# An adaLN block on one core: the probabilities of tiles 8 and 16 turned by a trip over DRAM instead of by TensorE

## What is computed

```python
mod = (_silu(L0_c) @ L0_wmod).reshape(L0_c.shape[0], 6, 1, -1)      # sa, ca, ga, sb, cb, gb
h = _layernorm(x, axis=-1) * (1 + ca) + sa
x = x + ga * _L0_attn_ref(h, L0_attn_Wq, L0_attn_Wk, L0_attn_Wv, L0_attn_Wo)
h = _layernorm(x, axis=-1) * (1 + cb) + sb
x = x + gb * _L0_ffn_ref(h, L0_ffn_factors, L0_ffn_bias)
```

## Time and profile before

| | us |
|---|---|
| median of 3 runs | 449.46 (448.65 to 449.9) |
| the profiled execution | 449.87 |
| its span in the trace | 448.1 |
| PE busy | 439.6 (98%) |
| DVE busy | 357.2 (80%) |
| ACT busy | 321.0 (72%) |
| POOL busy | 235.3 (53%) |

### The profile page before, as it was taken

How to read it: one execution, slowest core, us unless ns; L and a number is a source line. 1 busy time by engine, 2 the same in 40 slices (tenths; PEclk the granted TensorE clock), 3 DMA queues, 4 the chain that set the end, 5 groups by cost and what they waited for, 6 DMA issues and landing times.

```text
span 448.1 us, 7294 instructions
## 1 busy us (share of the span) xinstructions
PE 439.6 (98%) x2118; PEld 361.5 (81%) x2118; DVE 357.2 (80%) x610; ACT 321.0 (72%) x642; POOL 235.3 (53%) x308
## 2 busy tenths in 40 slices
PE   8899999999999999999999999999999999999996
PEld 7586888878888888878888888888888888787885
DVE  5687657768887889978897888888886788999977
ACT  3677557778797786788877787778887673767651
POOL 1453516852565645355565545455564526077982
PEclk9999999999999999999999999999999999999999
DMA  8999976533676467667676367766676047558423
GB/s 317 392 385 290 251 151 111 125 120 98 195 221 191 132 195 229 200 181 242 194 250 191 116 203 234 223 192 220 199 236 210 25 152 207 183 173 278 130 79 140
DMA packets 77750, 88.05 MB, mean 197 GB/s; under 512 B 5000, under 2 KB 55944, under 8 KB 77200
## 3 DMA queue, kind: packets, MB, share of 16 engines
q1 hardware_dynamic: 73872, 80.51, 56.4%
q0 software_dynamic: 3264, 6.29, 7.8%
q10 hardware_dynamic: 576, 0.79, 0.5%
HBM read 53.49 MB, written 34.10 MB: 195 GB/s over the span
## 4 chain that ended last, share of the span: by engine, by line
PE 75%; DVE 11%; issue 4%; ACT 3%; POOL 3%; DMA 2%; DVEq 0%; POOLq 0%; SPq 0%
PE ps_o L524 9%; PE ps_o L526 9%; PE ps_o L525 9%; PE ps_v L524 6%; PE ps_v L525 5%; PE ps_v L526 5%; PE ps_y L526 4%; PE ps_y L524 4%; PE ps_y L525 4%; PE ps_qk L524 3%; PE ps_qk L525 2%; PE ps_qk L526 2%; PE ps_s L603 2%; PE ps_s L604 2%; DVE pt_lo L1194 2%
## 5 line engine op out<-in xcount | busy, mean ns | idle before, releaser
L1674 POOL TENSOR_SCALAR ve<-mv 128x1 f32<-128x1 f32 x64 | 16.5, 257 | 159.2 <-DVE mv L1309 118.2
L524 PE MATMUL ps_o<-v_lo,pt_hi 128*128 128x512 f32 x192 | 74.8, 389 | 0.6 <-DVE pt_lo L1194 0.6
L525 PE MATMUL ps_o<-v_hi,pt_lo 128*128 128x512 f32 x192 | 74.7, 389 | 0.0
L526 PE MATMUL ps_o<-v_hi,pt_hi 128*128 128x512 f32 x192 | 74.7, 389 | 0.0
L1194 DVE TENSOR_TENSOR h_lo<-h_f,h_hi 128x512 fp32r<-128x512 f32 x57 | 41.7, 731 | 28.7 <-ACT h_hi L832 28.4
L860 ACT ACTIVATE h_f<-x1b,mod_t 128x128 f32<-128x128 f32 x120 | 53.2, 596 | 3.8 <-DVE x1b L1327 3.8
L1676 POOL TENSOR_TENSOR rstd<-ve,minus_half 128x1 f32<-128x1 f32 x64 | 46.5, 727 | 5.3
L524 PE MATMUL ps_v<-wvo_lo,h_hi 128*128 128x512 f32 x112 | 44.7, 399 | 0.7 <-DVE h_lo L1194 0.7
L525 PE MATMUL ps_v<-wvo_hi,h_lo 128*128 128x512 f32 x112 | 43.7, 391 | 0.0
L526 PE MATMUL ps_v<-wvo_hi,h_hi 128*128 128x512 f32 x112 | 43.7, 390 | 0.0
L524 PEld LDWEIGHTS ps_o<-v_lo,pt_hi 128*128 128x128 f32 x192 | 36.0, 188 | 8.5 <-issue 1.0
(11 more groups left out here) (232 smaller groups left out, 1191.3 us busy)
## 6 DMA issues: line engine op xcount, KB each, us to landing
x_blocks<-xn SPq DMA_DIRECT2D x50, 256.0 KB, 2.7
p_blocks<-probs SPq DMA_DIRECT2D x24, 512.0 KB, 3.7
pb<-p_blocks SPq DMA_DIRECT2D x96, 128.0 KB, 2.8
x1b<-x_blocks SPq DMA_DIRECT2D x30, 256.0 KB, 2.8
result<-x_ring SPq DMA_DIRECT2D x15, 512.0 KB, 3.0
xb<-x_blocks SPq DMA_DIRECT2D x20, 256.0 KB, 3.0
x_ring<-in_x SPq DMA_DIRECT2D x18, 256.0 KB, 3.9
wmod<-in_wmod SPq DMA_DIRECT2D x4, 1024.0 KB, 15.7
```

Source lines behind the costliest of these rows:

```text
L524: nc.tensor.matmul(acc, a_hi, b_lo, start=first, stop=False)
L525: nc.tensor.matmul(acc, a_lo, b_hi, start=False, stop=False)
L526: return nc.tensor.matmul(acc, a_hi, b_hi, start=False, stop=last)
L1674: nc.gpsimd.tensor_scalar(ve[:, one], mv[:, u, 1:2], EPS, None, ALU.add).then_inc(ve_done, 1)
```

## The change

Tiles 8 and 16 are turned by the trip (`opens_by_trip`); tile 24 stays with PE. In steps 7 and 15 the scores of the opening tile stand ahead of the feed-forward, and DVE takes qk_lo and k_both (the keys' rests) directly behind the residual sum. Its exponential stands first among what ACT does behind the two pt_hi, and send and fetch are moved forward in SP's order. In steps 7, 8, 15 and 16 ACT handles x's columns (modulate, round) ahead of x1's. In steps 8 and 16 DVE turns the probabilities directly behind the first row maximum.

```diff
@@ -24,7 +24,11 @@
 
 
 def turned_by_pe(t):
-    return t <= LAST_EARLY or t % PER_BATCH == 0
+    return t <= LAST_EARLY or t == TILES - PER_BATCH
+
+
+def opens_by_trip(t):
+    return t % PER_BATCH == 0 and not turned_by_pe(t)
 
 
 def pe_turns_of(t):
@@ -454,19 +458,25 @@
                     fetch_x(t + TB + 1, 1 - u)
                 if opening is not None:
                     send_p(opening)
-                if t + 1 < T and not turned_by_pe(t + 1):
+                if t + 1 < T and not turned_by_pe(t + 1) and not opens_by_trip(t + 1):
                     fetch_p(t + 1)
+                if opens_by_trip(t + 1):
+                    send_p(t + 1)
                 if 1 <= t < T - 1:
                     send_x1(t - 1, 1 - u)
-                if u and g >= 2:
+                if opens_by_trip(t + 1):
+                    fetch_p(t + 1)
+                if u and g >= 2 and not opens_by_trip(t + 1):
                     store_pair(g - 2)
                 if 1 <= t < T - 1:
                     fetch_x1(t - 1, 1 - u)
+                if opens_by_trip(t + 1):
+                    store_pair(g - 2)
                 if t < T - TB and t % TB in (2, 4):
                     spread_gate(t % TB // 2 - 1, t // TB + 1)
                 if 12 <= t + TB + 2 < T:
                     send_x(t + TB + 2, u)
-                if scored_in(t) is not None and not turned_by_pe(scored_in(t)):
+                if scored_in(t) is not None and not turned_by_pe(scored_in(t)) and not opens_by_trip(t + 1):
                     send_p(scored_in(t))
                 if 2 * TB <= t + TB + 3 < T and t >= 5:
                     sp.wait_ge(y_stored, 16 * ((t - 5) // 2 + 1))
@@ -694,9 +704,11 @@
                     late_x()
                 if t:
                     project_values(t + TB, u)
+                if opens_by_trip(t + 1):
+                    scores_of(t + 1)
                 if t >= 3:
                     feed_forward(t - 3)
-                if scored_in(t) is not None:
+                if scored_in(t) is not None and not opens_by_trip(t + 1):
                     scores_of(scored_in(t))
                 if ready is not None:
                     ready()
@@ -994,6 +1006,8 @@
                 if scored_last_in(t - 1) is not None:
                     exponentials(scored_last_in(t - 1))
                 probs_part(t, 0)
+                if opens_by_trip(t):
+                    probs_part(t, 1)
                 if u:
                     qk(g + PB)
                 if q in late_x_banks:
@@ -1003,20 +1017,28 @@
                 if parts is not None:
                     parts(0)
                 values(t + TB)
-                probs_part(t, 1)
+                if not opens_by_trip(t):
+                    probs_part(t, 1)
+                if opens_by_trip(t + 1):
+                    exponentials(t + 1)
                 if parts is not None:
                     parts(1)
-                if t:
+                around = opens_by_trip(t) or opens_by_trip(t + 1)
+                if t and not opens_by_trip(t):
                     normalize_x1(t - 1, 1 - u, q < T)
-                if t >= 3:
+                if t >= 3 and not around:
                     modulate_x1(t - 2, batch_of((t - 2) // 2))
                 if q < T and q not in late_x_banks:
                     modulate_x_turned(q, batch_of(q // 2))
                 if q < T and t != 2:
                     h_upper(q, 1 - u)
+                if opens_by_trip(t):
+                    normalize_x1(t - 1, 1 - u, q < T)
+                if around:
+                    modulate_x1(t - 2, batch_of((t - 2) // 2))
                 if beside is not None:
                     beside()
-                if scored_in(t) is not None:
+                if scored_in(t) is not None and not opens_by_trip(t + 1):
                     exponentials(scored_in(t))
                 if behind is not None:
                     behind()
@@ -1336,25 +1358,38 @@
                 q = t + TB + 1
                 if scored_last_in(t - 1) is not None:
                     row_max(scored_last_in(t - 1))
+                if opens_by_trip(t):
+                    turn_p(t)
                 if t:
                     add_x(t - 1)
+                if opens_by_trip(t):
+                    probs_rest(t, 0)
+                    probs_rest(t, 1)
+                if opens_by_trip(t + 1):
+                    qk_rest(g + PB)
+                    k_rest(g + PB)
+                if t:
                     x1_stats(t - 1, 1 - u)
-                if u:
+                if u and not opens_by_trip(t + 1):
                     qk_rest(g + PB)
                 if t >= 3:
                     turn_x1(t - 2)
-                if u:
+                if u and not opens_by_trip(t + 1):
                     k_rest(g + PB)
-                probs_rest(t, 0)
+                if not opens_by_trip(t):
+                    probs_rest(t, 0)
                 if t == 2:
                     h_rest(q, 1 - u)
                 if between_halves is not None:
                     between_halves()
-                probs_rest(t, 1)
+                if not opens_by_trip(t):
+                    probs_rest(t, 1)
                 values(t + TB)
+                if opens_by_trip(t + 1):
+                    row_max(t + 1)
                 if q < T and q not in late_x_banks:
                     turn_x(q)
-                if scored_in(t) is not None:
+                if scored_in(t) is not None and not opens_by_trip(t + 1):
                     row_max(scored_in(t))
                 if t == 2:
                     turn_x1(0)
@@ -1369,7 +1404,7 @@
                     x_moments(q + 1, u)
                 if q < T and t != 2:
                     h_rest(q, 1 - u)
-                if not turned_by_pe(t + 1):
+                if not turned_by_pe(t + 1) and not opens_by_trip(t + 1):
                     turn_p(t + 1)
                 if t >= 2:
                     h2_rest(t - 2)
```

## The result

| | before | after |
|---|---|---|
| median, us | 449.50 (448.65 to 449.90, 4 runs) | 455.68 (455.04 to 456.19, 4 runs) |
| ratio, 95% interval | | 1.0134 (1.0106 to 1.0161) |
| profiled execution, its span | 449.87, 448.1 | 456.19, 454.4 |

A forecast was written before the change was run, and what follows sets the result against it. PE, busy 98% of the span, was taken as the bound. Around tile 8 +1.15 and tile 16 +1.8, the 1.76 gain included, make +2.95 on 449.46: 452.4 us, range 449.0 to 455.4.

The forecast's parts named there:

- 0.88 us a tile won: On PE, removing a tile's eight transposes saves 0.88 us, 1.76 us for both tiles.
- The trip of tile 8 is just hidden: Step 8: turned probabilities arrive at 161.7, DVE comes to them at 161.75; the trip costs 0 to 0.2 us.
- DVE's lateness in step 8: ACT idles until 152.2; h2_lo starts at 158.5, not 156.27, and the row maximum at 160.6, not 158.75.
- h_lo of tile 17 ends at 170.9, wait 1.2: Step 9: PE wants h_lo at 169.7 for queries and keys, so it waits 1.2 us, more than the 0.88 gained.
- The probabilities of tile 9 are there soon enough: Their send goes out about 2 us later than 161.24; they land at about 171, in time for what follows.
- The first pt_lo of tile 9 takes 0.69: Step 9 on DVE: starts 178.7, ends 179.4, making the attention of tile 9 1.05 us late.
- Tile 16, 1.8 us: Around tile 16 PE ends 1.8 us later, with no wait there to absorb any of it.
- 0.66 us absorbed at step 11: PE's earlier 0.66 us wait before step 11's queries and keys absorbs part of 1.8 us, leaving +1.15 around tile 8.
- The lateness and its cause: DVE's queue is late by 1.9 us from ACT's idle stretch and 1.17 us from the turn of the probabilities.
- Draw: Rival: only step 9's wait at the queries comes, 1.2 against 0.88, DVE catches up; 449.4 us; chance 0.19.
- full gain: Rival: the chains have slack, no waits come; 447.7 us, half of it 448.6; chance 0.15 in full or part.
- late trip: Rival: tile 8's probabilities land after DVE reaches them, 2.15 us late; 456.7 us, or 454.6 for one tile; chance 0.08.

The follow-up runs named there:

- e13: Changed kernel with ACT modulating x1's columns ahead of the exponential of tiles 8 and 16 in steps 7 and 15; ratio 1.0123 to the kernel before.
- e16: e13 with SP's store ahead of fetching tile 8's probabilities, and the send of tile 9's probabilities ahead of fetching x of tile 17; ratio 1.0137.
- e4: Changed kernel with SP's store of the finished pair put ahead of the fetch of the opening tile's probabilities; ratio 1.0121 to the kernel before.
- e5: Changed kernel with POOL's operations for tile t-4 held back in steps 9 and 17 until both pt_lo are done; ratio 1.0131 to the kernel before.
- e3: Changed kernel with eight dummy matmuls ahead of PE's wait for h_lo in step 9; ratio 1.0134 to the kernel before.
- e7: Changed kernel with the new order kept but no trip, PE transposing tiles 8 and 16 again; ratio 1.0113 to the kernel before.
- e17: e16 with the first pt_lo ahead of x1's statistics on DVE in steps 9 and 17; ratio 1.0105 to the kernel before.
- e8: Changed kernel with the store order of e4 and POOL held back as in e5; ratio 1.0125 to the kernel before.
- e2: Changed kernel with the trip for tile 16 only, tile 8 turned by PE in the old order; ratio 1.0061 to the kernel before.
- e15: e7 with x1's columns modulated ahead of the exponential on ACT, as in e13; ratio 1.0047 to the kernel before.
- e6: Changed kernel with x1's columns ahead of x's on ACT again, as in the kernel before; ratio 1.0159 to the kernel before.

## Why the prediction was right in direction and wrong in size

- *0.88 us a tile won.* Nearly: the attention of tile 8 comes 0.71 earlier.
- *The trip of tile 8 is just hidden.* Right: turn at 162.05 without idle time, forecast 161.75. Not "just": its data were there at 160.79, and with the 0.54 the forecast would be 162.24. What hides it is DVE's lateness in part: with DVE 1.6 us earlier, counted from the queries of step 7 (e13), the trip is 0.31 late, and 1.87 only in e16, where the store stands in front of its fetch.
- *DVE's lateness in step 8.* Right to some tenths: h2_lo 159.03 (forecast 158.5), row maximum 160.91 (160.6); all of after stands 0.54 later. ACT idle 2.71 ahead of the exponential (forecast 3).
- *h_lo of tile 17 ends at 170.9, wait 1.2.* Too low: 172.5, wait 1.97. x landed 0.75 late, and this h_lo took 1.13, beside POOL, which the sum left out knowingly. With x in time (e4, e5) the wait is 0.73, less than forecast.
- *The probabilities of tile 9 are there soon enough.* Wrong: 1.15 late in after, 1.10 in e4, 1.44 in e13. On SP their send stood behind the fetch of x, at 164.31 where I had about 163.2.
- *The first pt_lo of tile 9 takes 0.69.* This is the step that failed. I took one slow half and put it second, though in the earlier trace rows both were slow (3.54 together). It was 3.3 to 3.5 in all traces in which neither it nor POOL was moved, and the attention of tile 9 was 2.3 to 3.1 late in after, e3, e4, e7 and e13; 0.64, 1.25 and 1.67 where POOL was elsewhere (e17, e5, e8). In after the first half took 1.67 us: of the 2.04 us by which the attention of tile 9 is later than forecast (3.09 against 1.05), 0.98 are this term, 0.92 the later start of that pt_lo (behind the waits for x of tile 17 and pb of tile 9), and 0.15 the clock. Tile 17, whose pair took 1.29 in after, shows the same within one run: its attention is 0.92 late (35.70 us behind the queries of step 15, before 34.78). I had the price (2 us for both tiles, 454.4) among the bounds and not in the sum. The Trainium skill (SBUF — State Buffer, Who interferes with whom) says that the later of the two instructions waits for the whole of the other; both halves at some 1.7 us beside two operations of POOL agree, and the rule was the better guide than my choice. It is the largest mistake, not the whole miss of 3.2 us: 0.54 lie ahead of step 7, and in tile 8's stretch (4.13, forecast 1.15) 0.94 more came in behind the attention of tile 9, in steps 10 and 11.
- *The clock* isn't in the forecast at all. 1.65 us were lost by it in after, nearly all beside DVE's lateness.
- *Tile 16, 1.8 us.* 1.49 in after, but 2.7 by time in e2 (2.44 in its stretch), paid at the queries for h_lo, as in the first step of the forecast, only larger.
- *0.66 us absorbed at step 11.* In e3, e4, e13 and e17, yes; in after no: DVE waited 2.06 us for x of tile 19 (2.23 before) and PE 0.56 again. That fetch took 4.77 us to land in after and 5.00 before, against 3.08 in e4 and 2.95 in e13. So the 0.66 goes with a slow fetch, and is no slack to count on.
- *The lateness and its cause.* The forecast blamed the turn (1.17) and ACT's slip (1.9) together. The order alone costs 5.1 and the trip on top about 1 (6.0 against 5.1; the intervals overlap), after paying back 1.76; e7 has a wait of its own, so the split is rough. The slip is the larger part of the order: 3.0 of the 5.1 by e15.
- *Draw, full gain, late trip.* None came in after. The late trip comes as soon as DVE is in time, by 0.31 us (e13), or by 1.87 with the store in front (e16).

Not settled: how much of the remaining 2.1 us of e15 its two waits make (its stretches show 0.92), and whether the new order costs anything ahead of step 7 or the first 20 us of a kernel just vary by that much.

## What to carry to other kernels

Work that is moved first in line of an in-order engine costs all who stand behind it the time that the engine then idles; look for something ready to run in that gap before looking at what the moved work itself costs. Where several chains are late by about the same, taking one away moves the wait to the next: with the trip, POOL, clock and slip each "won" 1 to 2 us at their place and nothing that the time shows. A wait read from one execution can also be that execution's own: compare traces in which nothing at that place was changed before giving it a cause. And when the rows show both of a pair slow, price both slow.

## Of the hardware

- A wait of about 2 us did or did not lower PE's clock: after waits of 1.97 us (after, 172.52) and 2.00 us (e6, 276.92) the granted clock was 0.71 and 0.70 in the next 5.8 us; after waits of 1.97 (e2, 276.48) and 1.99 us (e6, 172.29) it stayed 1.00. After 2.25 us (e13, 277.03) it stayed 1.00 too, and after 3.09 us (e5, 277.63) it was 0.50 in the next 2.9. So the length of the wait alone doesn't tell whether the clock falls.
- With a store of results ahead of the four fetches of one tile's probabilities these had landed 5.5 to 5.7 us after the first issue (e4, e16), against 4.1 (after, e13).
- The fetch of x of one tile (128x512) took between 2.5 and 5.4 us to land in these traces (2.54 before, 5.38 in e5).
- The first 20 us of a kernel, the same in all, take up to 1.6 us longer (e2) than in the profiled execution of before.
- VectorE's subtraction of 128x512 with both inputs in SBUF took 0.69 us alone and 1.65 to 1.83 beside GpSimd's operations of 128x512 (pt_lo of tile 9).
